# A second FFN block moved to the end of the seventh slot and the third to the eighth

## The reference

```python
def ffn_layer(x, g, bln, W1, b1, W2, b2):
    mu = x.mean(-1, keepdims=True)
    var = ((x - mu) ** 2).mean(-1, keepdims=True)
    xn = (x - mu) / jnp.sqrt(var + 1e-05) * g + bln
    hg = xn @ W1 + b1
    a, gate = jnp.split(hg, 2, -1)
    return a * jax.nn.gelu(gate, approximate=False) @ W2 + b2
for i in range(DEPTH):          # DEPTH = 6
    x = attn_layer(shift_tokens(x), Wqkv[i], q_scale[i], k_scale[i], Wo[i]) + x
    x = ffn_layer(shift_tokens(x), ln_g[i], ln_b[i], W1[i], b1[i], W2[i], b2[i]) + x
```

## Time and profile before

| what | value |
|---|---|
| median of 3 runs | 2512.11 us (2511.95 to 2513.39) |
| profiled execution, its own time | 2515.83 us |
| its span, first to last instruction | 2513.9 us |
| mean granted TensorE clock | 0.961 |
| PE busy | 2312.5 us (92%) |
| DVE busy | 1766.0 us (70%) |
| POOL busy | 1598.5 us (64%) |
| ACT busy | 1373.6 us (55%) |
| DMA, all queues | 83.91 MB, 33 GB/s mean |

### The profile page before, as it was taken

How to read it: one execution, slowest core, us unless ns; L and a number is a source line. 1 busy time by engine, 2 the same in 40 slices (tenths; PEclk the granted TensorE clock), 3 DMA queues, 4 the chain that set the end, 5 groups by cost and what they waited for, 6 DMA issues and landing times.

```text
span 2513.9 us, 81640 instructions
## 1 busy us (share of the span) xinstructions
PE 2312.5 (92%) x34944; PEld 1575.0 (63%) x34944; DVE 1766.0 (70%) x2707; ACT 1373.6 (55%) x2778; POOL 1598.5 (64%) x931
## 2 busy tenths in 40 slices
PE   5668999999999999999999999999987988889998
PEld 3435666666666666666666666666655766656665
DVE  2348788877888778887788778887756888832232
ACT  1115666666666666666666666666644666643332
POOL 0039889888898888888888888988843222201111
PEclk8879999999999999999999999999987899989999
DMA  4001111111121112211121112211122000000000
GB/s 111 0 9 37 30 35 51 49 43 30 34 58 50 33 32 51 53 37 31 33 62 48 33 30 58 52 33 35 30 58 64 1 1 1 1 1 5 5 5 5
DMA packets 77303, 83.91 MB, mean 33 GB/s; under 512 B 24964, under 2 KB 48786, under 8 KB 76946
## 3 DMA queue, kind: packets, MB, share of 16 engines
q1 hardware_dynamic: 76946, 78.70, 12.2%
HBM read 26.56 MB, written 1.07 MB: 11 GB/s over the span
## 4 chain that ended last, share of the span: by engine, by line
PE 49%; DVE 29%; issue 12%; ACT 7%; POOL 3%; SPq 0%; ACTq 0%; DMA 0%; POOLq 0%; DVEq 0%
PE bank L613 7%; DVE n L1222 6%; DVE qk L1215 6%; PE bank L532 5%; ACT qk L908 4%; PE bank L625 4%; PE sbank L569 3%; PE bank L633 3%; DVE sh L1235 3%; DVE mx L1231 3%; PE bank L821 2%; PE obank L831 2%; PE sbank L831 2%; PE obank L602 2%; PE sbank L821 2%
## 5 line engine op out<-in xcount | busy, mean ns | idle before, releaser
L1215 DVE TENSOR_TENSOR qk<-bank,tab 128x1024 f32<-128x1024 f32 x384 | 469.2, 1222 | 212.5 <-ACT qk L908 212.4
L1528 POOL TENSOR_TENSOR qk<-qk 128x1024 f32<-128x1024 f32 x192 | 454.3, 2366 | 188.5 <-DVE qk L1215 188.3
L1532 POOL TENSOR_TENSOR rn<-n2m,cst 128x16 f32<-128x16 f32 x192 | 562.8, 2931 | 16.0
L532 PE MATMUL bank<-wqk,xs 128*128 128x512 f32 x768 | 409.2, 615 | 2.6 <-DMA xs<-Z 0.9
L908 ACT ACTIVATE qk<-bank 128x512 f32<-128x512 f32 x384 | 226.5, 590 | 300.5 <-PE bank L532 300.5
L1536 POOL TENSOR_TENSOR qk<-qk,rn 128x1024 f32<-128x1024 f32 x192 | 365.4, 1903 | 28.1 <-POOL rn L1532 0.9
L543 PEld LDWEIGHTS bank<-cst,qk 128*128 128x128 f32 x1536 | 191.5, 141 | 215.6 <-issue 170.4
L1540 POOL TENSOR_TENSOR lnr<-lnv,cst 128x2 f32<-128x2 f32 (+1 forms) x88 | 66.4, 754 | 394.1 <-DVE lnv L1110 394.1
L543 PE MATMUL bank<-cst,qk 128*128 128x128 f32 x1536 | 231.8, 274 | 11.3 <-POOL qk L1536 11.3
L1222 DVE TENSOR_REDUCE n<-qk 128x16 f32<-128x1024 f32 x192 | 232.1, 1209 | 0.0
L553 PE MATMUL lnbank<-wv,xs 128*64 128x512 f32 x768 | 208.0, 620 | 0.0
(11 more groups left out here) (201 smaller groups left out, 4332.6 us busy)
## 6 DMA issues: line engine op xcount, KB each, us to landing
vp<-vp SPq DMA_DIRECT2D x672, 65.0 KB, 2.0
wqk<-in_L_ffn_Wqkv SPq DMA_DIRECT2D x24, 256.0 KB, 3.7
wv<-in_L_ffn_Wqkv SPq DMA_DIRECT2D x6, 512.0 KB, 4.0
wo<-in_L_ffn_Wo SPq DMA_DIRECT2D x6, 512.0 KB, 4.2
xs<-Z SPq DMA_DIRECT2D x48, 64.0 KB, 2.0
xs<-Z SPq DMA_DIRECT2D x48, 63.8 KB, 2.7
vp<-in_L_ffn_w SPq DMA_DIRECT2D x1, 2048.0 KB, 13.1
mw<-in_L_ffn_w SPq DMA_DIRECT2D x8, 256.0 KB, 6.9
```

What stands on the lines that cost most here:

```text
L532: nc.tensor.matmul(bank[s % 2][:, :], xs[:, odd, WIN + r * P:WIN + r * P + P], wqk[:, lo:lo + 512], start=True, stop=True).then_inc(p_full, 1)
L1215: tt(qk[:, both, :].rearrange("p o (h d) -> p o h d", d=DH), heads(bank[c % 2][:, :]).unsqueeze(1).broadcast_to([P, 2, PAIRS, DH]), table. ...
L1528: tt(direct, direct, swapped, ALU.add).then_inc(sum_done, 1)
L1532: tt(rn[:, m % 2, :], n2m[:, :], const("mhalf"), ALU.pow).then_inc(rn_done, 1)
```

## The change

In step t, for item f = t-2:

- PE: hidden(f, 1) goes from behind turn(t, 2) in s=6 to the end of s=6, behind turn_probs(i, 3). hidden(f, 2) goes from the end of s=6 to s=7, between turn(t, 3) and weigh(i, 3).
- ACT: gelu(f, 1) goes from s=6 to the start of s=7; gelu(f, 2) from the start of s=7 to behind take_turned in s=7, and exps(t, 0) stands behind it.
- DVE: gate(f, 0) goes from behind norms in s=5 to behind parts(t, 6) in s=6; gate(f, 1) from there to the start of s=7; gate(f, 2) from the start of s=7 to behind parts(t, 7).

```diff
@@ tensor: step @@
-                    if s in (5, 6) and p2:
-                        hidden(f, s - 5)
+                    if s == 5 and p2:
+                        hidden(f, 0)
+                    if s == 7 and p2:
+                        hidden(f, 2)
...
                     if s == 6 and p2:
-                        hidden(f, 2)
+                        hidden(f, 1)
@@ scalar: step @@
                     if s == 7 and p2:
-                        gelu(f, 2)
+                        gelu(f, 1)
...
+                    if s in (5, 7) and p2:
+                        gelu(f, s - 5)
                     if s == 7 and p0:
                         exps(t, 0)
-                    if s in (5, 6) and p2:
-                        gelu(f, s - 5)
@@ vector: step @@
                     if s == 7 and p2:
-                        gate(f, 2)
+                        gate(f, 1)
                     if p0:
                         parts(t, s)
                     if s == 4 and p2:
                         scale_norm(f)
-                    if s == 6 and p2:
-                        gate(f, 1)
+                    if s in (6, 7) and p2:
+                        gate(f, 2 * (s - 6))
...
-                    if s == 5 and p2:
-                        gate(f, 0)
```

## The result

The changed kernel takes 2528.64 us (median of 4 runs, 2528.41 to 2528.84), beside 2512.68 us before (2511.95 to 2513.39). The ratio is 1.0063 with a 95% interval of 1.0047 to 1.0079: slower by 0.63%, 16.0 us. The prediction was 2532.3, range 2517 to 2541. The profiled execution takes 2528.84 us with a span of 2526.9, clock 0.965; before it was 2515.83 and 2513.9.

A forecast was written before the change was run, and what follows sets the result against it. PE was taken as the bound, only its standing time counting. Removing the 0.88 us wait and adding later waits and late weights summed to +0.44 us per item, 46 times +20.2 us: 2532.3 us, range 2517 to 2541.

The forecast's parts named there:

- What bounds the kernel: PE bounds the items; waiting for gate 0 costs 0.88 us per item, so reordering could return at most 40 us.
- The wait removed and the waits added: From turn(t, 2): 0.88 us gained; then 0.34 lost at turn_out, 0.60 at hidden 1, 0.18 waiting at hidden 2.
- the choice of 0.61 behind seed: DVE in s=7: gate 1 was taken to start 0.61 us after seed's start, where the old row had 0.68.
- The surcharge for late weights behind hidden 2: In s=7, weights that could not be loaded ahead add 0.10 us between hidden 2 and weigh.
- the sum of 0.44: Next item's projection starts 0.44 us later in each item; over 46 items, +20.2 us.
- Tail: Steps 48 and 49, after the full items: change put at 0, from -1 to +1 us.
- Rival 1: Hidden 2 in s=7 does not wait for gate 1: +0.16 us per item, +7.4 us, 2519.5 us; chance 0.12.
- Rivals 2 and 3: Gate 0 ends 0.60 us sooner: 2487 us, chance 0.07; some 0.3 us sooner: within 5 us of 2512, chance 0.07.
- Rival 4: Clock falls to 0.64 from turn(t, 2) to next projection: +5.6 us per item, 2769 us; chance 0.02.
- Rival 5: Late weights after turn_out, longer second wait, contract waiting 0.2 for gate 2: 0.81 us per item, 2549 us; chance 0.06.

## Why the prediction was right

*What bounds the kernel.* Right: wherever the clock stayed at 1.00, the period measured follows from where PE stands. With all waits for gates taken out it fell from 35.11 to 34.27, by 0.84 of the 0.88 that was given as the most. The rest are the new neighbours of hidden 1: turn_out follows it after 0.96, where a projection follows after 0.86, and turn_probs follows turn_out after 0.44 instead of 0.49.

*The wait removed and the waits added.* Right, each at its place. From turn(t, 2) on, expected and measured after: turn_out 1.66 and 1.66, hidden 1 3.19 and 3.18, projection 4.15 and 4.15, hidden 2 5.63 and 5.62, next projection 9.89 and 9.84. The chain norms, reciprocal, ao, parts, gate 0 ran in exactly its distances, and the choice of 0.61 behind seed was right (1035.22 to 1035.83).

*The mis-sized term.* The surcharge for late weights behind hidden 2. The sum took 0.10, from the second block, which has 128 columns of weights; hidden 2 has 85. Measured, hidden 2 to weigh is 1.02 (1036.36 to 1037.38), 1.02 or 1.03 in all items, instead of 1.06: a surcharge of 0.06 to 0.07. It doesn't hang on how late the block is: with gate 0 back in s=5 hidden 2 starts 0.47 late and pays the same (1036.76 to 1037.79), and with hidden 1 behind scores it starts 0.41 late and pays 0.07 (1018.39 to 1019.32, packed 0.86). The loads of the weights of the two kinds of block take 192 and 155 ns on average after the change (the number behind the busy time):

```profile
L625 PEld LDWEIGHTS bank<-lnt,w 128*128 128x128 f32 x384 | 66.2, 192 | 39.8 <-DVE hT L1274 32.5 <-DVE lnt L1268 2.1
L625 PEld LDWEIGHTS bank<-lnt,w 128*85 128x85 f32 x192 | 26.0, 155 | 20.9 <-DVE hT L1274 14.7 <-issue 0.3
```

So the sum of 0.44 was 0.04 too high; an item costs 0.40, and 46 of them 18.4 us where 20.2 were forecast.

*Tail.* Put at 0, within 1 us. It gained 1.2 us: from the last contract but two to the last but one it is 25.85 us before and 24.62 after. Before, hidden 1 of step 48 waited 1.9 us and the clock fell to 0.64 behind it; after, turn_out and turn_probs stand ahead of hidden 1, two waits of 1.0 and 1.1 us take the place of the 1.9, and the same stretch of the step has a clock of 1.00 (second row of the table by stretches above). That the edit did this is not shown. In step 48 the run with hidden 1 behind scores has PE's order of before and the same wait, yet its clock stayed at 1.00 and this distance is 24.62 too (in the profiles of the three other runs with that wait it is 25.81 to 25.86, as before):

```profile
1842.25 1.13 PE L625 MATMUL bank<-lnt,w 128*128 128x256 f32 x4 [1.91 <-DVE hT L1274]
```

```profile
1842.20:1846.60 4.40, 3.89 (x80) 2.84 (x80) 1.78 (x5) 1.98 (x4) 0.00 (x0) 1.00 0.00 0
```

So the order of step 48 is worth 0, as forecast, when the clock stays up, and the 1.2 us are what the clock loss costs there. Whether the two shorter waits prevent that loss, or the profiles after just did not have it, is open.

*The rest.* 18.4-1.2 = 17.2 us by that count; the last residual of the profiles is 16.5 us later, less by 0.3 because the first contract comes at 257.99 us where it was at 258.30; the medians differ by 16.0. Of the 4.2 us by which the forecast increase of 20.2 was too large, the surcharge is 1.8 and the tail 1.2, if the other executions had it as the profiled one. The span itself grew by only 13.0: the blocks behind the items, in which nothing was edited, take 624.2 us before and 620.7 after at a mean clock of 0.92 and 0.93:

```profile
1889.70:2513.90 624.20, 544.33 (x3400) 390.20 (x3399) 344.42 (x661) 295.73 (x813) 126.75 (x92) 0.92 0.02 6
```

```profile
1906.20:2526.90 620.70, 539.43 (x3400) 386.00 (x3399) 344.41 (x661) 295.53 (x813) 126.66 (x92) 0.93 0.02 6
```

In the kernel with DVE's old order under the changed PE they take 616.8 us at 0.94, with the same 3400 matmul records. So some 7 us of a time come from the clock in blocks that the edit doesn't touch, and 1 or 2 us between medians of this kernel say nothing of the items. What sets that clock in one profile and not in another was not tried.

*The rivals.* Rival 1 (second wait hidden) is refuted by the start of hidden 2, 0.06 behind gate 1. Rivals 2 and 3 needed gate 0 to start sooner than 1.13 behind parts; it did not. Rival 4 did not come, but the run with gate 0 later still shows it at a wait of 2.5 us, in two items of five. Rival 5 needed contract to wait; it is packed at 1.01 behind values.

## What to carry to other kernels

Where blocks share one buffer and pass between three queues, moving a block later on the engine that waits paid here where the operation that it waits for stayed in its place: the PE move by one operation of 0.79 us covered the wait of 0.78, while moving block and gate together carried the wait along. Walk each in-order queue from the last point that nothing moves, with start-to-start distances of the trace, and look at what is late next: the longest wait of the list could be removed here without winning anything. A move that is worth nothing alone may be worth its full sum behind another one, so the two are to be measured together too.

## What the runs showed of the hardware

A stop of PE of 2.47 us in each item made the granted clock fall to about one half in two items of every five (periods 40.26 and 38.92 beside 37.32 us); in the first of the two it stayed there for some 6 us. In the other three the same stop left it up. In step 48 a stop of 1.9 us was followed by 0.64 before the change and by 1.00 in the run with hidden 1 behind scores, and one of 2.74 us by 1.00 in the run with gate 0 back in s=5 (stretch 1877.1 to 1882.3 us). So the length of a stop alone doesn't say whether the clock falls. Stops of up to 0.66 us, two in an item, left it at 1.00 (the same run). A matmul group whose weights had to wait with it took 0.10 us longer with 128 columns of weights and 0.07 with 85, the latter whether it was 0.17, 0.41 or 0.47 us late.
